# Three of eight output additions of a quad move from VectorE to ScalarE and GpSimd

## The reference

```python
x, gate = split(hidden @ W_in.T)            # 2048 + 2048 channels
x = silu(causal_conv4(x) + conv_b)
ts, Bm, Cm = rms(split(x @ W_x.T))          # 64, 16, 16
dt = softplus(ts @ W_dt.T + b_dt)
state = state * exp(dt * A) + dt * x * B_t  # per token, 16 states a channel
y = sum_n(state * C_t) + x * D
y = (y * silu(gate)) @ W_out.T
x1 = layernorm(hidden + y)
```

## Time and profile before

| | |
|---|---|
| median of 3 runs | 2970.67 us (2968.34 to 2972.52) |
| the profiled execution | 2971.96 us, of which span 2969.9 us |
| mean granted TensorE clock | 0.968 |
| busy: TensorE, VectorE | 92%, 86% |
| busy: GpSimd, ScalarE | 65%, 57% |
| instructions | 35293 |

### The profile page before, as it was taken

How to read it: one execution, slowest core, us unless ns; L and a number is a source line. 1 busy time by engine, 2 the same in 40 slices (tenths; PEclk the granted TensorE clock), 3 DMA queues, 4 the chain that set the end, 5 groups by cost and what they waited for, 6 DMA issues and landing times.

```text
span 2969.9 us, 35293 instructions
## 1 busy us (share of the span) xinstructions
PE 2729.3 (92%) x11120; PEld 1557.2 (52%) x11120; DVE 2552.7 (86%) x3525; ACT 1695.5 (57%) x2848; POOL 1922.2 (65%) x886
## 2 busy tenths in 40 slices
PE   8988899999989999998999887888889999999996
PEld 4444555555555555555555454555544555555553
DVE  2289999999999999999999999999966787787785
ACT  2366556565665657566565654756534555555553
POOL 1179798888969889896988988889731222222221
PEclk9998999999999999999999999889899999999998
DMA  5352333433343343334333333322401211111110
GB/s 173 132 123 72 112 104 95 136 116 110 91 152 105 94 135 120 107 99 144 110 93 97 100 87 94 121 87 65 113 29 38 97 56 56 64 56 56 64 60 26
DMA packets 132876, 281.32 MB, mean 95 GB/s; under 512 B 12528, under 2 KB 12656, under 8 KB 132224
## 3 DMA queue, kind: packets, MB, share of 16 engines
q1 hardware_dynamic: 132736, 279.59, 31.1%
HBM read 245.86 MB, written 33.69 MB: 94 GB/s over the span
## 4 chain that ended last, share of the span: by engine, by line
PE 54%; DVE 32%; issue 8%; ACT 4%; POOL 1%; DMA 0%; DVEq 0%; POOLq 0%; SPq 0%; ACTq 0%
DVE arena L1429 17%; PE banks L524 16%; PE banks L548 9%; DVE arena L1445 7%; PE banks L618 7%; PE banks L764 4%; PE banks L717 4%; PE banks L673 3%; PE banks L698 3%; PE banks L561 2%; PE banks L688 2%; PE banks L728 2%; ACT banks L1166 1%; DVE arena L1376 1%; PE banks L771 1%
## 5 line engine op out<-in xcount | busy, mean ns | idle before, releaser
L1344 POOL TENSOR_TENSOR arena<-arena 128x2048 f32<-128x2048 f32 x255 | 1158.6, 4544 | 78.5 <-PE banks L618 78.5
L1429 DVE TENSOR_TENSOR_SCAN arena<-banks,arena 128x512 f32<-128x512 f32 x1024 | 1184.7, 1202 | 14.9 <-POOL arena L1344 8.9
L1166 ACT ACTIVATE banks<-arena,a_sb 128x508 f32<-128x508 f32 x1024 | 696.8, 684 | 727.9 <-DVE arena L1429 724.2
L524 PE MATMUL banks<-arena 128*128 128x512 f32 x2048 | 954.6, 603 | 11.4 <-DMA arena<-in_xT 8.2
L618 PEld LDWEIGHTS banks<-ident,arena 128*128 128x128 f32 x4096 | 490.4, 145 | 396.7 <-issue 177.4
L618 PE MATMUL banks<-ident,arena 128*128 128x128 f32 x4096 | 572.5, 283 | 115.1 <-DVE arena L1445 64.1
L524 PEld LDWEIGHTS banks<-arena 128*128 128x128 f32 x2048 | 373.0, 195 | 363.1 <-issue 358.8
L1445 DVE SCALAR_TENSOR_TENSOR arena<-banks,cg,arena 128x512 f32<-128x512 f32 x640 | 452.4, 737 | 76.4 <-PE banks L618 75.8
L548 PE MATMUL banks<-arena 128*128 128x512 f32 x1024 | 472.9, 601 | 5.7 <-DMA arena<-in_WoutT 4.4
L1276 POOL TENSOR_TENSOR arena<-arena 128x512 f32<-128x512 f32 x240 | 306.9, 1279 | 207.2 <-ACT arena L910 204.8
L1357 POOL TENSOR_TENSOR arena<-arena 128x512 f32<-128x512 f32 x128 | 141.4, 1104 | 431.9 <-DVE arena L1610 431.8
(11 more groups left out here) (139 smaller groups left out, 2973.3 us busy)
## 6 DMA issues: line engine op xcount, KB each, us to landing
arena<-b_scratch SPq DMA_DIRECT2D x128, 512.0 KB, 5.1
arena<-in_WinX SPq DMA_DIRECT2D x128, 256.0 KB, 2.8
arena<-in_WinZ SPq DMA_DIRECT2D x128, 256.0 KB, 2.7
arena<-in_WoutT SPq DMA_DIRECT2D x32, 1024.0 KB, 5.9
u_scratch<-arena SPq DMA_DIRECT2D x64, 256.0 KB, 5.1
arena<-u_scratch SPq DMA_DIRECT2D x16, 1024.0 KB, 9.5
arena<-x_scratch SPq DMA_DIRECT2D x32, 512.0 KB, 3.4
arena<-in_xT SPq DMA_DIRECT2D x14, 1024.0 KB, 8.2
```

What stands on the lines that cost most here:

```text
L524: last = nc.tensor.matmul(home(kind, i), wr[w % 2][:, k, :], x[:, k, :], start=(k == 0), stop=(k == KC - 1))
L1166: nc.scalar.activation(by_seq(bank(i % 2))[:, :, 1:SEQ], by_seq(dt[s % 2][:, i, :])[:, :, 1:SEQ], ACT.Exp, scale=a_sb[:, QD * q + i, n:n + ...
L1344: nc.gpsimd.tensor_tensor(hb[n % 4].rearrange("p (i t) -> p i t", i=QD), dtu, brep[pair % 3][:, n % 2:n % 2 + 1, :].broadcast_to([P, QD, G ...
L1429: nc.vector.tensor_tensor_scan(h, bank(i % 2), h, 0.0, ALU.mult, ALU.add)\
```

## The change

In quads 1 to 10 the chains O0, O1 and O2 are no longer added by VectorE. ScalarE copies the bank to one new buffer `stage` (new function `act_out`, 128x512), and that frees the bank. GpSimd adds `stage` to `rbuf` (new function `pool_out`). ScalarE's copies stand in its steps 9, 10, 11 (late: 5, 6, 7) behind the fourth decay, GpSimd's adds in its steps 11, 12, 14 (late: 7, 8, 9). The buffer `part2` is cut from two copies to one, which makes the room for `stage`. VectorE keeps O3 to O7 at their old places.

```diff
+STAGED = 3
-FREED = {"X": "conv_done", "Z": "z_exp", "O": "r_added", "D": "dt_ok", "Y": "fin", "P": "ph_ok"}
+FREED = {"X": "conv_done", "Z": "z_exp", "D": "dt_ok", "Y": "fin", "P": "ph_ok"}
+def staged(i):
+    return i % 8 < STAGED and has_x(i // 8 + 1)
+def stages(i):
+    return sum(staged(j) for j in range(i))
...
-        part2 = at(3072, 2, QD * P)
+        part2 = at(3072, QD * P)
+        stage = at(3584, HALF)
...
-                pe.wait_ge(S[FREED[kind]], i + 1)
+                if kind == "O" and staged(i):
+                    pe.wait_ge(S["o_copied"], stages(i) + 1)
+                elif kind == "O":
+                    pe.wait_ge(S["r_added"], i + 1 - stages(i))
+                else:
+                    pe.wait_ge(S[FREED[kind]], i + 1)
...
+        def act_out(act, s, c):
+            i = 8 * (s - 1) + c
+            act.wait_ge(S["o_mm"], i + 1)
+            after(act, "r_pooled", stages(i))
+            nc.scalar.activation(stage, home("O", i), ACT.Copy).then_inc(S["o_copied"], 1)
...
-                after(act, "sum2_ok", (len(SHARED) - 1) * s + k - 2)
-                dst = part2[:, k % 2, :]
+                after(act, "sum2_ok", (len(SHARED) - 1) * s + k - 1)
+                dst = part2
...
+            if mine and s > 0 and e in ((23, 27, 31) if q == NQ - 1 else (39, 43, 47)):
+                act_out(act, s, e // 4 - (5 if q == NQ - 1 else 9))
...
+        def pool_out(pool, s, c):
+            i = 8 * (s - 1) + c
+            h, b = divmod(c, GB)
+            v = rbuf[:, b, h * HALF:(h + 1) * HALF]
+            if c == 0 and (s - 1) % NQ == 0:
+                pool.wait_ge(S["r_loaded"], 16 * ((s - 1) // NQ + 1))
+            pool.wait_ge(S["o_copied"], stages(i) + 1)
+            after(pool, "r_added", 8 * (s - 1) - stages(8 * (s - 1)))
+            after(pool, "r_pooled", stages(8 * (s - 1)))
+            nc.gpsimd.tensor_tensor(v, stage, v, ALU.add).then_inc(S["r_pooled"], 1)
...
+                if s > 0 and mine and n in ((7, 8, 9) if q == NQ - 1 else (11, 12, 14)):
+                    pool_out(pool, s, ((7, 8, 9) if q == NQ - 1 else (11, 12, 14)).index(n))
...
-                for c in range(7):
+                for c in range(STAGED if mine else 0, 7):
                     if n == ((3, 4, 4, 5) if late else (7, 8, 9, 9))[c] if c < 4 else n == (14, 15, 15)[c - 4]:
                         dve_out(dve, s, c)
```

More of the change, by code:

```diff
@@ L124 @@
 dt_mm dt_abs dt_exp dt_ln dt_ok dtu_part dtu_ok cg_ok exp_ok bm_part bm_ok scan_ok t_done acc_ok part_ok sum_ok part2_ok sum2_ok yt_mm fin1 fin
-z_mm z_copied z_exp z_ln z_sig z_ok o_mm r_added ln_stats ln_aggr ln_eps ln_rstd ln_shift ln_ok x1_stored
+z_mm z_copied z_exp z_ln z_sig z_ok o_mm o_copied r_pooled r_added ln_stats ln_aggr ln_eps ln_rstd ln_shift ln_ok x1_stored
 p2_const wv_loaded ones_set ph_mm ph_ok gs_ok cn_loaded ct_loaded x1_loaded xres_loaded out_stored
@@ L1283, in pool_sums2 @@
             after(pool, "sum2_ok", (len(SHARED) - 1) * s + k - 1)
-            nc.gpsimd.tensor_tensor(acc2, acc2, part2[:, k % 2, :], ALU.add).then_inc(S["sum2_ok"], 1)
+            nc.gpsimd.tensor_tensor(acc2, acc2, part2, ALU.add).then_inc(S["sum2_ok"], 1)
+        def pool_out(pool, s, c):
[8 more added lines that the diff above has]
+            nc.gpsimd.tensor_tensor(v, stage, v, ALU.add).then_inc(S["r_pooled"], 1)
         def pool_u(pool, m):
@@ L1453, in dve_out @@
             v = rbuf[:, b, h * HALF:(h + 1) * HALF]
-            if c == 0 and (s - 1) % NQ == 0:
+            if c == (STAGED if has_x(s) else 0) and (s - 1) % NQ == 0:
                 dve.wait_ge(S["r_loaded"], 16 * ((s - 1) // NQ + 1))
             dve.wait_ge(S["o_mm"], i + 1)
-            after(dve, "r_added", 8 * (s - 1))
+            after(dve, "r_added", 8 * (s - 1) - stages(8 * (s - 1)))
+            after(dve, "r_pooled", stages(8 * (s - 1)))
             nc.vector.tensor_tensor(v, home("O", i), v, ALU.add).then_inc(S["r_added"], 1)
         def dve_ln_tile(dve, g, t):
-            dve.wait_ge(S["r_added"], 8 * NQ * (g + 1))
+            dve.wait_ge(S["r_added"], 8 * NQ * (g + 1) - stages(8 * NQ * (g + 1)))
+            dve.wait_ge(S["r_pooled"], stages(8 * NQ * (g + 1)))
             for h in range(2):
@@ L1801, in _ @@
             pe.wait_ge(S["ones_set"], 1)
-            pe.wait_ge(S["r_added"], 8 * NS)
+            pe.wait_ge(S["r_added"], 8 * NS - stages(8 * NS))
             pe_sequence(pe, 0, keys=True, tail=False)
```

## The result

| | before | after |
|---|---|---|
| median | 2971.30 us (4 runs) | 2991.36 us (2988.06 to 2995.09, 4 runs) |
| the profiled execution | 2971.96, span 2969.9 | 2994.16, span 2992.4 |

The ratio is 1.0069 [1.0052, 1.0087]: 20 us slower. The four runs lie in two pairs, 2988.06 and 2988.56 at a mean clock of 0.967, 2994.16 and 2995.09 at 0.964 and 0.963, and the profile, which is of the second, is compared by its own time; why there are two pairs stays open.

A forecast was written before the change was run, and what follows sets the result against it. GpSimd's unbroken run, which holds all three new adds, was taken to gate the scans and transposes Y. 22.7 − 1.2 + 6 = 27.5 us slower gave a median of 2998 us, range 2983 to 3011.

The forecast's parts named there:

- the clock's 6 us: A longer TensorE wait before transposes Y slows its clock: 1.0 us in each of six quads, 6 in all.
- all three places named: Waiting on GpSimd's run: VectorE's scans of state 13 (slack 1.43 us), of state 16 (0.97), and TensorE's transposes Y (0.10).
- The sum without the clock: Ordinary quads lose 6 × 3.02 + 2 × 2.3 = 22.7 us, late quads gain 1.2: 21.5.
- 2.25 − 1.43 and 3.48 − 0.97: Products' delay less slack: state 13's scans start 0.85 us later, state 16's 2.55, as the prediction stated.
- The wait before Y: TensorE's idle time before the transposes Y in an ordinary quad grows from 0.54 to 3.6 us.
- the whole 3.02: State 15's sum on GpSimd, hence the transposes Y, comes 3.02 us later, passed on in six quads.
- the clock holds: Rival: GpSimd's run delays ordinary quads as forecast, but TensorE's clock doesn't drop; 21.5 us slower, 2992; chance 0.25.
- Late quads: Quads 3 and 7: TensorE's wait of 2.03 us shrinks by about 0.6, gaining 2 × 0.6 = 1.2 us.
- the cost is nothing: Quads 3 and 7: GpSimd's three adds, 3.70 us, fit into its own waits; without these, up to 3.7.
- The cover: GpSimd's waits of 3.98 and 1.83 us in quad 3, together taken as enough for its adds of 3.70.
- counted at nothing: ScalarE's three copies, 1.76 us a quad against 47 idle, cost below 0.1 us and were taken as nothing.
- The most to be won: Ordinary quad: VectorE stands about 0.8 us behind TensorE, so sparing it adds wins at most about 0.75 us.

The follow-up runs named there:

- two-input dummies alone: Kernel before, single `part2`, with three more GpSimd adds a quad on scratch, reading two different buffers; VectorE keeps all its adds: 2997.98 us, ratio 1.0087.
- one add at Y: Kernel before, single `part2`, one dummy two-buffer GpSimd add for each of eight ordinary quads, directly ahead of state 15's sum: 2974.46 us, ratio 1.0010.
- that run: The changed kernel without GpSimd's 30 new adds, ScalarE's copies kept: 2960.94 us, ratio 0.9966.
- the last two versions: The change in quads 3, 7; in 1, 2, 5, 6, 9, 10 only O0, GpSimd adding in next step 4; ScalarE's copy in step 10 (2967.35 us) or 9 (2965.30 us).

## Why the prediction came out as it did

- **The time.** Predicted 2998, 27 us slower; measured 2991.36, 20 slower, inside the range. Without the clock's 6 us the sum was right.
- **The bound** was right. GpSimd's unbroken run, not its share of 65%, decides, at all three places named. Only GpSimd's load, with VectorE untouched, gives the whole loss.
- **The sum without the clock** was 21.5 against 21.59 measured. The add was taken at 1.235; it steps by 1.22 to 1.23. 2.25 − 1.43 and 3.48 − 0.97 are 0.82 and 2.51, where 0.85 and 2.55 were stated, which moves the sum by less than 0.1. The Trainium skill (GPSIMD Engine Reference, sections 4.1 and 3.1) was right to speak against the change, and the trace nearly agrees with its ratio of 1.96: 1.27 over 0.673 is 1.89.
- **The wait before Y** was predicted at 3.6 and is 1.71. The step that failed: I put the whole 3.02 there and also let step 11 grow by 0.85, as if the two were apart. What TensorE already stood back at step 11 and in the turn of 0.51 no longer shows at Y. The total per quad was right, its place was not.
- **The clock**, 6 us at Y, failed both as a place and as a size. It was hung on the 3.6. The waits there are 1.71 and 0.95, and no stretch at Y is slowed. Stretches at 1.2 GHz came behind the 2.1 of step 11, and GpSimd's backlog covers them. The rival "the clock holds" names the right time, 2992, but by its words only in part the right reason: the clock did fall, at a place where it cost nothing. That transposes suffer less from the half clock was misread too. The eight of 1.31 us at 833.25 ran at a clock of 1.00, ahead of the slowed stretch, and the same 1.31 stands at 557.99 above at full clock. At 1.2 GHz eight transposes take 1.95 for 1.04 (quad 5 above). The Trainium skill (TensorE: Matmul & The Clock Gate, "What's actually happening") has the throttled state as the default, released by activity, and I took from it that a slower stretch behind Y was due every time. The wait of 3.6 that this was to follow never came, so no run here tests it at Y.
- **Late quads.** −1.29 for −1.2, by luck. Quad 3 won 1.28 because it has no slowed stretch now. Its wait of 2.03 is now 1.08, but that the stretch went with the wait isn't shown: the runs with two-input dummies alone and with one add at Y keep the wait of 2.02 to 2.03 in quad 3 and have no slowed stretch there either. Quad 7 won 0.4, not 0.6. From Y to Y it takes 129.01 us (1091.28 to 1220.29) for 129.43; the 0.01 of the table has the border in it. The step "the cost is nothing" failed: it costs 0.3. The cover had been read without VectorE's earlier arrival, which shortens it, and in the disturbed quad.
- **ScalarE** was counted at nothing. Its copy in step 9 delays the logarithm of dt, and takes 0.2 of what O0's add gives VectorE (0.40 with the copy a step later). In the whole change GpSimd's backlog hides that.
- **The most to be won** in an ordinary quad was put at 0.75, from VectorE's lag. Measured, 0.53. The 0.2 of ScalarE's copy, which that run has in step 9 too, would make up the rest; this is an estimate, no run shows it.

## What to carry to other kernels

Before work is moved to an engine with a low share, lay its timeline beside the deadlines of what it feeds, and find the stretch in which it never waits. An instruction there costs its full length to everyone behind, whatever it spares elsewhere; the same instruction ahead of that engine's next wait costs nothing. Read a cover from the undisturbed instance of a pattern and reckon with its shrinking where the change makes another engine come earlier. Put a delay into the sum once, where it first appears. And when stretches are compared, look at where their borders stand.

## What I had not expected of the hardware

- A GpSimd add of 128x512 float32 takes 1.05 us when both inputs are one buffer and 1.28 when they are two.
- Eight waits of 2.09 to 2.11 us before the same 16 short matmuls were followed by the half clock five times and by the full clock three times. With two chains such waits had four stretches behind eight of them, with the two-input dummies alone five behind eight. Two stretches of the kind also came behind such waits of 1.65 in the run with only GpSimd's load. In all runs in which that wait was 1.25 or less (before, one chain and one add at Y among them) quads 1 to 10 have none behind it.
- Quads 12 to 15, the same instructions in every kernel here, take either 479.1 to 479.5 or 474.2 to 474.7 us together. The kernel before has 479.29, the one after 479.12, the one without GpSimd's adds 474.68. The slowed stretches fall on other matmuls; why is open. The step of 4.5 us is as large as the gain of either of the last two versions, so a change this small has to be read by quad.
